# A graph-attention, expert and graph-convolution kernel: gates in front of the next tile's transposes, identity products at the start, and the weight transposes two counting steps later

## The reference

```python
x = x + gat(layernorm(x), src, dst, W, attn_l, attn_r, W_res)   # 12 heads of 64, softmax over edges
x = x + experts(layernorm(x), Wg, bg, W1, b1, W2, b2)           # argmax of 4 gates, one expert per node
x = x + gcn2(layernorm(x), W1, b1, W2, b2, edges)               # two graph convolutions
x = x + ffn(layernorm(x), w_fc, b_fc, w_proj, b_proj, alphas)
```

## Time and profile before

| | us |
|---|---|
| median of 3 executions | 1025.79 |
| lowest and highest | 1024.16, 1026.54 |
| profiled execution, its own time | 1026.78 |
| its span in the trace | 1025.0 |
| TensorE busy in the span | 977.4 (95%) |
| VectorE busy | 597.7 (58%) |
| ScalarE busy | 312.9 (31%) |
| mean granted TensorE clock | 0.985 |

### The profile page before, as it was taken

The page is one execution under the profiler, slowest core; times in us unless marked ns, Lnnn a source line. Parts: engine busy times, 40 slices in busy tenths (PEclk is TensorE's granted clock), DMA queues, the critical chain, the costliest instruction groups (busy, mean ns, idle before and its releaser), DMA issues.

```text
span 1025.0 us, 15765 instructions
## 1 busy us (share of the span) xinstructions
PE 977.4 (95%) x5652; PEld 790.6 (77%) x5652; DVE 597.7 (58%) x1264; ACT 312.9 (31%) x888; POOL 67.5 (7%) x134
## 2 busy tenths in 40 slices
PE   7999999999999999996899997999999999999997
PEld 5777678999999999984566654667997557878785
DVE  8887799999999999994223236541111112333331
ACT  2444354665555666443111121221111110110100
POOL 2100000000000000132122210000000000000000
PEclk9999999999999999998899998999999999999999
DMA  6000010111111111026762538123001005111002
GB/s 160 2 1 1 1 55 13 38 39 37 49 42 47 46 37 37 13 70 237 241 239 90 185 123 287 46 67 127 1 1 47 0 1 161 37 31 31 31 0 61
DMA packets 40018, 70.01 MB, mean 68 GB/s; under 512 B 21074, under 2 KB 24926, under 8 KB 39448
## 3 DMA queue, kind: packets, MB, share of 16 engines
q1 hardware_dynamic: 37321, 58.85, 18.2%
q0 software_dynamic: 2080, 10.23, 3.0%
q10 hardware_dynamic: 559, 0.16, 0.1%
HBM read 50.10 MB, written 19.12 MB: 68 GB/s over the span
## 4 chain that ended last, share of the span: by engine, by line
PE 89%; DVE 4%; issue 2%; DMA 2%; ACT 1%; POOL 0%; ACTq 0%; POOLq 0%; DVEq 0%; SPq 0%
PE O L952 19%; PE pw L1117 15%; PE pc L831 8%; PE pa L1145 7%; PE O L949 6%; PE pw L1178 6%; PE ph L1043 5%; PE py L1064 5%; PE pa L1190 3%; PE pf L796 3%; PE pw L1204 2%; PE pf L831 2%; PE O L898 1%; PE pt L1107 1%; PE pct L808 1%
## 5 line engine op out<-in xcount | busy, mean ns | idle before, releaser
L952 PE MATMUL O<-X,masks 125*125 125x264 f32 x1200 | 277.5, 331 | 0.0
L949 PE MATMUL O<-X,CSR 125*125 125x132 f32 x1080 | 244.1, 226 | 0.0
L952 PEld LDWEIGHTS O<-X,masks 125*125 125x125 f32 x1200 | 220.1, 186 | 0.1
L1762 DVE SCALAR_TENSOR_TENSOR masks<-a2b,NA,CSR 125x375 fp32r<-125x375 f32 (+1 forms) x360 | 212.2, 651 | 6.4 <-PE O L952 4.9
L949 PEld LDWEIGHTS O<-X,CSR 125*125 125x125 f32 x1080 | 203.3, 188 | 0.0
L2023 DVE SCALAR_TENSOR_TENSOR UL<-pw,dinv,UH 125x768 fp32r<-125x768 f32 x20 | 20.4, 1018 | 111.0 <-ACT UH L1496 111.0
L1117 PE MATMUL pw<-W 128*125 128x384 f32 x240 | 81.5, 497 | 1.0 <-ACT W L1489 1.0
L831 PE MATMUL pc<-ohs_a,ohd 125*125 125x512 f16 x375 | 77.9, 347 | 1.6 <-DVE ohs_a L1572 1.6
L1117 PE MATMUL pw<-region,xr_or_h 128*125 128x384 f32 x240 | 77.6, 486 | 0.0
L1117 PEld LDWEIGHTS pw<-W 128*125 128x125 f32 x240 | 45.4, 193 | 32.3 <-issue 3.6
L1117 PEld LDWEIGHTS pw<-region,xr_or_h 128*125 128x125 f32 x240 | 45.1, 188 | 32.1
(11 more groups left out here) (248 smaller groups left out, 1418.9 us busy)
## 6 DMA issues: line engine op xcount, KB each, us to landing
a2b<-a_rows SPq DMA_DIRECT2D x12, 610.4 KB
W<-in_L_ffn_W SPq DMA_DIRECT2D x4, 1152.0 KB
WM<-in_L_ffn_W SPq DMA_DIRECT2D x4, 1152.0 KB
xr_or_h<-in_x SPq DMA_DIRECT2D x10, 336.0 KB
XH<-in_x SPq DMA_DIRECT2D x12, 280.0 KB
z_rows<-region SPq DMA_DIRECT2D x10, 336.0 KB
region<-y_rows SPq DMA_DIRECT2D x10, 336.0 KB
x_rows<-xr_or_h SPq DMA_DIRECT2D x10, 336.0 KB
```

Source lines behind the costliest of these rows:

```text
L949: nc.tensor.matmul(O[0:P, bank, d - d0, 2 * DP:4 * DP], CSR[:, s, d * P:(d + 1) * P], X[:, buf, s, 4:6, :].rearrange("p k d -> p (k d)"), ...
L952: ins = nc.tensor.matmul(O[0:P, bank, d - d0, 0:4 * DP], kept, X[:, buf, s, 0:4, :].rearrange("p k d -> p (k d)"), start=s == 0, stop=s == ...
L1762: nc.vector.scalar_tensor_tensor(masks[:, s, 0:(d1 - d0) * P], a2b[:, buf, d0 * P:d1 * P], NA1[:, s, bass.ds(h, 1)], CSR[:, s, d0 * P:d1 * ...
```

## The change

The identity products write to a part of the PSUM tile `pf` that is written again before it is read. They wait for `ident` alone. `turn_projections` stands ahead of step 5 in place of step 3. `gates(0)` stands ahead of `turn_z(1)`, and ScalarE's `copy_zt(0)` ahead of its `z_of(1)`.

```diff
             def _(pe):
+                def warm_up(n):
+
+                    for _ in range(n):
+                        nc.tensor.matmul(pf[:, 2, 0:128], ident[:, :], ident[:, :], start=True, stop=True)
+
                 pe.wait_ge(s_ident, 2)
+                warm_up(2)
                 pe.wait_ge(s_ef, 1)
                 for n in range(4):
                     nc.tensor.transpose(pct[0:P, n * 85:n * 85 + 85], edgef[:, n, :],
                                         ident[0:85, 0:85]).then_inc(s_et, 1)
+                warm_up(3)
...
-                    if n == 3:
+                    if n == 5:
                         turn_projections()
...
                     pe.wait_ge(s_wg, 32)
-                    for t in range(NT):
+                    gates(0)
+                    turn_z(1)
+                    for t in range(1, NT):
                         if t + 1 < NT:
                             turn_z(t + 1)
                         gates(t)
-                        if t:
-                            turn_gates(t - 1)
+                        turn_gates(t - 1)
                     turn_gates(NT - 1)
...
+                    copy_zt(0)
                     z_of(1)
-                    copy_zt(0)
                     evict(H - 1, 1, 2)
                     gates_of_tiles()
```

## The result

| | us |
|---|---|
| changed, median of 14 executions | 1025.03 (1023.80 to 1026.40) |
| before, median of 14 beside them | 1026.62 (1024.16 to 1028.85) |
| ratio, 95% interval | 0.9982, 0.9974 to 0.9990 |
| profiled execution: own time, span | 1023.95, 1022.2 |

The kernel is faster by 0.18%, 1.0 to 2.7 us by the interval. Timed once more in another set the changed kernel had 1025.43 against 1027.04, ratio 0.9990 (0.9980 to 1.0000), whose end touches no change. The medians lie 1.6 us apart in both sets. The two profiled executions differ by more, 1026.78 - 1023.95 = 2.83 us.

A forecast was written before the change was run, and what follows sets the result against it. TensorE, 89% of the chain that ended last, was taken as the bound. From 1026.78, 1.7 us at the start and 1.4 at the gates gave 1023.7; the middle between that and 1022.7 was 1023.2, range 1021.6 to 1025.6.

The forecast's parts named there:

- the step to the median: Going from the profiled execution to the median: the middle of 1022.7 and 1023.7 was taken, 1023.2.
- the two terms: The gains expected at two places: 1.7 us at the start and 1.4 us at the gates.
- the case in which both gains arrive: Start and gates both gain as summed; chance 50%, own range 1022.4 to 1024.0 us.
- the first rival: At the start the clock goes up no sooner: 0.1 us gained there, 1.4 at the gates, 1024.8 us; chance 15%.
- what can't be told from none: The outcome "same", a measured change of no more than 0.2% either way; chance 0.38.
- The products' cost: Identity products at the start: 0 taken as their delay; one takes 0.22 to 0.24 us, 0.45 to 0.48 at half.
- Step 18's end: At the start, TensorE would end step 18 at 22.7 us against 24.37, 1.7 gained.
- lower bound: Least gain at the start, 0.1 us: clock up at 14.8 as before, steps 3 and 4 at half speed ending at 12.5.
- The clock at the start: TensorE, at work nearly without a break from 3.1 us, would reach the full level between 6.5 and 9.5.
- The gates: Two gaps of 1.0 us replace 2.26, clock held: 1.4 us gained, 1.3 of it clock and 0.1 order.
- The rival that before's other executions don't have the fall: The clock's fall at the gates is missing in most executions of before: 0.1 us gained there, 1024.0 us; chance 15%.

The follow-up runs named there:

- gap filled: Kernel before plus nine unused identity products behind tile 0's transposes at the gates, order unchanged; 1026.55 us in its timed execution, gates 26.09 us.
- table early: Changed kernel plus a one-column ScalarE copy ahead of its wait for the weights' transposes, loading the function table earlier; 1024.50 us, ratio to before 0.9975.
- two banks: Changed kernel with two PSUM places, used in turn, for the transposes at the gates; 1024.00 us, ratio to before 0.9976.
- both: Changed kernel with the function table loaded early and two PSUM places for the gates' transposes; 1023.77 us, ratio to before 0.9973.
- products only: Kernel before plus the five identity products, weights' transposes still at step 3, gates as before; 1025.60 us, ratio to before 0.9988.
- start only: Changed kernel with the old gates order put back, keeping the identity products and the transposes at step 5; 1026.24 us, ratio to before 0.9992.
- changed again: The changed kernel, unaltered, profiled and timed a second time in another set; 1025.43 us, ratio to before 0.9990.
- gates only: Kernel before with only the new order of TensorE and ScalarE at the gates, start unchanged; 1026.45 us, ratio to before 0.9994.
- the first experiments: The earlier follow-up runs, timed beside the kernel before; the text doesn't list which ones are meant.
- ScalarE's half: Kernel before with only ScalarE's new order at the gates, copying tile 0 first; 1025.79 us in one timed execution beside 1027.68.
- before again: The kernel before, unaltered, timed against itself; 1027.74 against 1027.43 us, ratio 0.9994.
- transposes at step 5 only: Kernel before with the weights' transposes moved from step 3 to step 5, no identity products, gates as before; 1026.17 us, ratio to before 0.9996.
- TensorE's half: Kernel before with only TensorE's new order at the gates, gates of tile 0 first; 1027.19 us in one timed execution beside 1027.68.

## Why the prediction was right, point by point

- **Time.** 1023.2 was forecast, 1025.03 measured, in the range. The sum was made from one profile and came out between the two profiles: 1023.7 was worked out for an execution like the profiled one, and the profiled execution of the changed kernel took 1023.95. What was off is the step to the median. I took 0.5 us off the sum, since before's median stood 0.99 under its profile; over 14 executions it stands at 1026.62, so the profile was typical, and I should have taken nothing off. The forecast difference (2.6 us) is within the measured interval of 1.0 to 2.7, near its end; the two terms as summed, 3.1, are above it. The median also lies outside 1022.4 to 1024.0, the range that I gave the case in which both gains arrive, and is nearer to the 1024.8 of the first rival, whose mechanism the profiles don't bear out. So the mechanism was right and the gain was put too high; that the point is inside the whole range owes something to its width. At 0.18% the change lies just inside what can't be told from none, to which I gave 0.38.
- **The products' cost.** Nothing ahead of the edge transposes: right (one-hots at 6.00). An identity product takes 0.24 us at the full level (2.18 / 9, in the gap-filled kernel) and 0.52 at half (1.56 / 3): I had 0.22 to 0.24 and 0.45 to 0.48.
- **Step 18's end.** 22.7 forecast, 23.12 measured, 1.25 us gained for 1.7. The chain is the one forecast, 3.94 us from the weights' transposes to `project_attention` for 3.88. Its first link was mis-sized: the load landed at 11.30, not 10.98, which is 0.32 of the 0.42 that is missing. The rest is two small ones: L765 takes 0.34 at the full level (L772, above), where I took half of 0.48, and I counted 7.78 from the chain's 16.59, while L773 starts at 16.52 in the timeline. Over all profiles the term is about 1.0 us. In its lower bound a half-speed step was put at 1.13, the length of a group with its modelled end; from start to start it is 1.05, so two moved steps end at 11.7 to 11.9 and not at 12.5.
- **The clock at the start.** I expected the full level between 6.5 and 9.5 from the products. It came by about 9 in the changed kernel's two profiles, but between 10 and 11 in table early, two banks, both and products only (by their step times), and between 11 and 12 in start only: two of seven. The claim that TensorE at work nearly without a break from 3.1 brings it by 9.5 fell. What the runs show is that with steps in the place of the wait at 10.2 it came before 12 in each of seven profiles, six with products and one without, while with the wait left and no products it came behind 14 in four of six. In the one profile with the wait left and products it came before 11. Which of the two edits does it isn't separated.
- **The gates.** 1.4 us forecast; 1.46 between the two profiles, 1.6 over nine (mean of 27.46, 27.72, 27.72, 27.68 and 27.50 against 25.98). Two gaps of 1.0 with the clock held, the second one the uncovered copy, 1.3 of it clock and 0.1 order: each as forecast, and shown by the filled gap. The rival that before's other executions don't have the fall is wrong: it fell in all five profiles with both engines in the old order and no filling, and in both profiles of half the edit.
- **What stays open.** By the traces the two terms sum to 1.0 + 1.6 = 2.6 us; the two timed comparisons give 1.8 (1.0 to 2.7) and 1.0 (0 to 2.1). Between the two terms nothing is lost (the 432.7 us above). From the second tile's hidden transposes (L1053 before) to the end of the span it takes 515.9 to 517.5 us in all 14 profiles, with the new gates order 516.5 in the mean of six and with the old one 516.8 in the mean of five, so nothing is given back there either. One stretch is left, from behind the last gate to those transposes, 31.7 to 33.2 us. The four profiles with the changed kernel's gates (changed, changed again, gates only, table early) take 32.7 in the mean, the five with the old ones 32.2. Most of the 0.5 comes from the first expert tile's products, where the clock rises again. The changed kernel's profile and that of table early:

```profile
489.76 6.04 PE L1051 MATMUL ph<-W,region 128*128 x12 [1.31 <-DVE region L1944]
488.83 7.09 PE L1051 MATMUL ph<-W,region 128*128 x12 [1.32 <-DVE region L1945]
```

These products take 7.0 to 7.1 us in gates only, table early and gap filled, and 5.5 to 6.3 in the other 11 profiles. That is three of the seven profiles in which the clock held at the gates, and none of the seven in which it fell. If it is so in general, some 0.4 to 0.5 us of the gates' gain is given back and 2.1 are left; that the one causes the other isn't shown. Much of the noise goes with the clock too. Of the 35 executions of the kernel before beside the first experiments, the five with a mean granted clock of 0.981 to 0.983 took 1027.5 to 1031.0 us, and the four with 0.987 took 1023.2 to 1026.8. Whether the timed gain is lower than the traces' beyond this isn't settled.

## What to carry to other kernels

A wait on TensorE costs its length, and where the clock falls in it, more behind it: here 2.26 us without work cost 1.4 more, and cutting it into two gaps of 1.0 saved just that. Look for the granted clock in the windows behind every gap before pricing an order. When a stall at a fixed external time (a load) is filled with work, ask what the filling delays at the slower level: two steps at 1.05 us held the weights' transposes up to 11.7 and 11.9, while the load was there at 10.3 to 11.3 in other executions. And a function table can be loaded while its engine has nothing else to do: at 5.41 the load cost nothing, since ScalarE had no work of the kernel until 11.54, and behind the weights' transposes its 1.28 us lay in the chain.

## What the runs showed of the hardware

The moment at which the clock goes up differs from execution to execution of the same code: `project_attention` started anywhere from 14.79 to 17.01 in six profiles of the same start. The Trainium skill (TensorE: Matmul & The Clock Gate, Part 1 on the HAM clock gate) says that it varies from run to run, and these six agree. The page gives 0.5 us either way for a test of its own; here the spread is wider: the clock was up before 10.1 in ScalarE's half (three steps in 3.16 us for 3.39) and only behind 15 in gap filled (at 14.23 three steps still take 2.51, for 1.81). The fall at the gates didn't vary: it came in all six profiles that had the one gap of 2.26 us (before, before again, start only, transposes at step 5 only, products only, TensorE's half), in the one with a gap of 1.91, and in none of the four with two gaps of 1.0.

The 3 KB load of the attention vectors was issued at 5.00 and landed at 11.30 in the changed profile, at 10.98 before, and no later than 10.27 in another: 5.3 to 6.3 us. In the changed profile the queue with the node rows moved 2.56 MB in the first 13 us and took 80% of the time of the 16 DMA engines; that the load waited behind them is argued from this, not tested. The function table takes 1.28 us to load, which agrees with the Trainium skill's 1283 ns (ScalarE: Activation LUTs, What ACT_TABLE_LOAD costs); in these traces the first activation starts right behind it.
